# Attention 0: first scores and the spread of reciprocals on two row groups of TensorE, half of the normalisation on ScalarE and GpSimd, 24 transfers a step

## What is computed

```python
attn = jnp.einsum('bnchw,bncyx->bnhwyx', q, k) * (1.0 / np.sqrt(head_dim))
attn = jax.nn.softmax(attn, axis=-1)          # over x only: 32 keys of one row y
out = jnp.einsum('bnhwyx,bncyx->bnchw', attn, v).reshape(b, c, h, w)
out = jnp.einsum('oc,bchw->bohw', out_w, out) + out_b[None, :, None, None]
return out + input
```

## Time and profile before

| | |
|---|---|
| median of 3 runs | 3805.63 us (3801.79 to 3808.67) |
| profiled execution | 3806.82 us |
| its span (first to last instruction) | 3805.1 us |
| stage B in it | 106 to 958 us |
| PE busy over the span | 83% |
| DVE / ACT / POOL busy over the span | 50% / 74% / 8% |
| granted TensorE clock, mean | 0.956 of 2.4 GHz |

### The profile page before, as it was taken

One profiled execution on the slowest core, in us unless ns is written; L12 is line 12 of the kernel. 1 busy time (PEld: TensorE's weight loads), 2 busy tenths in 40 slices (PEclk: granted clock), 3 DMA queues, 4 the chain that ended last, 5 costly groups with the idle time before them and its releaser, 6 DMA issues.

```text
span 3805.1 us, 79261 instructions
## 1 busy us (share of the span) xinstructions
PE 3175.7 (83%) x27829; PEld 1180.1 (31%) x27829; DVE 1904.7 (50%) x2497; ACT 2817.5 (74%) x2759; POOL 300.4 (8%) x304
## 2 busy tenths in 40 slices
PE   5799999998773888888888888888888888779999
PEld 3344444444441222222222222222222222244443
DVE  3588878787575444444444444444444444452222
ACT  4444444444345999999999999999999999514555
POOL 5000000000354000000000000000000000001000
PEclk9899999999776999999999999999999999978999
DMA  5411111110143000000000000000000000200000
GB/s 186 115 40 47 48 44 47 48 32 10 38 144 124 17 16 17 17 17 17 17 17 17 17 16 16 16 17 17 17 17 17 17 17 16 72 17 6 11 14 14
DMA packets 118100, 134.09 MB, mean 35 GB/s; under 512 B 27246, under 2 KB 83660, under 8 KB 117964
## 3 DMA queue, kind: packets, MB, share of 16 engines
q1 hardware_dynamic: 117964, 132.29, 12.6%
HBM read 70.31 MB, written 55.57 MB: 33 GB/s over the span
## 4 chain that ended last, share of the span: by engine, by line
PE 57%; ACT 23%; issue 8%; DVE 5%; POOL 3%; SPq 1%; DMA 1%; ACTq 1%; DVEq 0%; POOLq 0%
ACT arena L878 22%; PE ps L1151 18%; PE ps L1128 10%; PE ps L989 3%; PE ps L1260 3%; PE ps L1267 3%; PE ps L1272 3%; PE ps L961 3%; PE ps L1007 2%; PE ps L1034 2%; PE ps L1009 2%; PE ps L1018 2%; DVE arena L1349 1%; POOL arena L698 1%; PE ps L1046 1%
## 5 line engine op out<-in xcount | busy, mean ns | idle before, releaser
L878 ACT ACTIVATE arena<-ps 128x1536 f32<-128x1536 f32 x1536 | 2063.8, 2095 | 11.0 <-PE ps L1128 11.0
L1151 PE MATMUL ps<-arena,Yall 128*32 128x512 f32 (+3 forms) x12288 | 1232.7, 496 | 10.8 <-POOL Yall L718 9.2
L1453 DVE TENSOR_TENSOR arena<-arena,causal 128x512 f32<-128x512 f32 x1024 | 674.3, 690 | 1043.4 <-ACT arena L878 1043.4
L1128 PE MATMUL ps<-Yall 15*128 15x512 bf16 (+3 forms) x6144 | 604.8, 330 | 396.7 <-ACT arena L878 373.8
L1128 PEld LDWEIGHTS ps<-Yall 15*128 15x128 bf16 x6144 | 163.2, 92 | 1277.3 <-ACT arena L878 1247.8
L803 ACT ACTIVATE arena<-ps 128x512 f32<-128x512 f32 x512 | 299.7, 595 | 293.3 <-PE ps L1009 283.8
L1151 PEld LDWEIGHTS ps<-arena,Yall 128*32 128x32 f32 x12288 | 284.1, 109 | 386.0 <-issue 360.4
L1349 DVE TENSOR_REDUCE arena<-ps 128x32 bf16<-128x1024 f32 x256 | 311.4, 1216 | 153.2 <-PE ps L989 153.2
L1356 DVE TENSOR_TENSOR arena<-arena,ps 128x512 f32<-128x512 f32 x512 | 329.2, 680 | 23.2 <-PE ps L1018 21.7
L1438 DVE COPY Yall<-ps 128x512 f32<-128x512 f32 x256 | 176.0, 688 | 198.3 <-PE ps L1151 198.3
L1009 PE MATMUL ps<-arena 128*128 128x256 bf16 x1024 | 257.5, 276 | 0.0
(11 more groups left out here) (172 smaller groups left out, 2083.8 us busy)
## 6 DMA issues: line engine op xcount, KB each, us to landing
Yall<-qstack SPq DMA_DIRECT2D x512, 30.0 KB
parts<-arena SPq DMA_DIRECT2D x8, 1536.0 KB, 5.9
arena<-parts SPq DMA_DIRECT2D x48, 256.0 KB, 5.4
arena<-parts SPq DMA_DIRECT2D x96, 128.0 KB, 2.8
Yall<-kstack SPq DMA_DIRECT2D x512, 24.0 KB
qstack<-arena SPq DMA_DIRECT2D x24, 384.0 KB, 3.2
attn<-Yall SPq DMA_DIRECT2D x512, 12.0 KB
arena<-arena SPq DMA_DIRECT2D x384, 16.0 KB, 1.8
```

The source lines that it names most:

```text
L878: act.activation(PR1[:, at:at + CW], bank(BPC * (kk % 2), BPC), ACT.Exp).then_inc(d_exp, 1)
L1128: mm = pe.matmul(bank(at + k)[:, s * P:(s + n) * P], Ks[par][HR * h:HR * h + QROWS, j * P:(j + 1) * P], Qs[par][HR * h:HR * h + QROWS, t * ...
L1151: mm = pe.matmul(o[HR * h:HR * (h + 1), :], Vg[par][:, j, 3 * h:3 * h + HR], pr[:, h * HALF + s * P:h * HALF + (s + n) * P], start=q < 2, ...
L1453: dve.tensor_tensor(v, v, m3, ALU.min).then_inc(d_mask, 1)
```

## The change

- First scores: two heads at once, one on array rows 0 to 31 (from `K1`), one on rows 32 to 63 (from `K2`), only the product of the high parts, half of the keys in each sub-step. Two matmuls of 512 columns as before, of 32 rows each.
- Spread: heads 0 and 1 on rows 0 to 47 into bank 4, heads 2 and 3 on rows 64 to 111 into bank 5; four matmuls of 48 rows and 256 columns in place of two of 96 rows and 512, all behind the first half of the scores. `RS` holds two half stacks, for the low and the high rows y.
- Normalisation: DVE multiplies heads 0 and 1 from bank 4. ACT copies bank 5 into one of two buffers in `sel`'s memory (`copy_spread`, between the two exponentials), and POOL multiplies heads 2 and 3 from there.
- Transfers: 24 of 16 partitions for each step, the 12 of the low rows y first, then the 12 of the high rows.
- ACT's exponentials stand ahead of the high and middle parts in sub-steps 3 and 4. POOL's low part stands in one list with its multiplications.
- POOL makes `sel` at the end of stage B, ahead of `V1`.

```diff
-        RS = [cut([NH0, QS], BF16) for _ in range(2)]
+        RS = [cut([2, 2, QS], BF16) for _ in range(2)]
...
+        spread_c = [flat_sel[:, k * HALF:(k + 1) * HALF] for k in range(2)]
+        spread = cut([SUB // 2, P], BF16)
...
@@ feed (SP)
-                    for r, part_made in enumerate((b_rhi, b_rmid, b_rlo)):
-
-                        sp.wait_ge(part_made, g + 1)
-                        for n in range(NH0):
-                            sp.dma_start(RS[st % 2][GK * r:GK * (r + 1), n, :], rec_parts[GK * n:GK * (n + 1), r, :])\
-                                .then_inc(rs_loaded[st % 2], INC)
+                    for y in range(2):
+                        for r, part_made in enumerate((b_rhi, b_rmid, b_rlo)):
+
+                            sp.wait_ge(part_made, g + 1)
+                            for n in range(NH0):
+                                to = P // 2 * (n // 2) + GH * r
+                                sp.dma_start(RS[st % 2][to:to + GH, y, n % 2, :],
+                                             rec_parts[GK * n + GH * y:GK * n + GH * (y + 1), r, :])\
+                                    .then_inc(rs_loaded[st % 2][y], INC)
@@ gpsimd
-            pool.memset(sel[0:NE, :, :], 0.0).then_inc(f_set, 1)
...
+            def pool_b(i, subs):
+                for k in subs:
+                    K = i * TURN + k
+                    if k % SUB == 4 and in_range(i, k, L_SUM + SUB + 2):
...
+                        pool.wait_ge(b_rmid, g + 1)
+                        wait_moved(pool, i, st - 1, 0)
+                        wait_moved(pool, i, st - 1, 1)
+                        pool.tensor_tensor(rec_parts[:, 2, :], rec_rest, rec_parts[:, 1, :],
+                                           ALU.subtract).then_inc(b_rlo, 1)
+                    if in_range(i, k, L_NORM):
+
+                        c = (k - L_NORM) % TURN
+                        e = E0[c // SUB % 2][:, c % SUB, 2:4, :].rearrange("p n q -> p (n q)")
+                        pool.wait_ge(b_copied, K + (1 - L_NORM))
+                        pool.tensor_tensor(e, e, spread_c[c % 2], ALU.mult).then_inc(b_norm_high, 1)
+            turns(pool, pool_b)
...
             pool.wait_ge(b_out, NSTEP)
+            pool.memset(sel[0:NE, :, :], 0.0).then_inc(f_set, 1)
...
             pool.memset(V1, 1.0).then_inc(ones_set, 1)
@@ scalar
+            def copy_spread(i, k, K):
+                if in_range(i, k, L_NORM):
+                    c = (k - L_NORM) % TURN
+                    act.wait_ge(b_spread_high, K + (1 - L_NORM))
+
+                    wait(act, b_norm_high, K + (-1 - L_NORM))
+                    act.activation(spread_c[c % 2], bank(5), ACT.Copy).then_inc(b_copied, 1)
@@ tensor
-                        for th in range(2):
-                            mm = pe.matmul(bank(th), Q1[q // 2][0:3 * D0, n, at:at + P],
-                                           half(K1[par][0:3 * D0, n, :], th), start=True, stop=True)
+                        for r, keys in enumerate((K1, K2)):
+                            mm = pe.matmul(bank(r), Q1[q // 2][D0 * r:D0 * (r + 1), n + r, at:at + P],
+                                           half(keys[par][D0 * r:D0 * (r + 1), n + r, :], th), start=True, stop=True)
...
-                        if in_range(i, k, L_NORM):
+                        if hp == 0 and in_range(i, k, L_NORM):
...
+                            for h in range(2):
+                                for G, made in enumerate((b_spread_low, b_spread_high)):
+                                    rows = slice(P // 2 * G, P // 2 * G + 3 * GH)
+                                    mm = pe.matmul(bank(4 + G)[:, h * QS:(h + 1) * QS], spread[rows, c % (SUB // 2), :],
+                                                   RS[c // SUB % 2][rows, c % SUB // (SUB // 2), h, :],
+                                                   start=True, stop=True)
...
-                        pe.wait_ge(b_norm, K * 2 + (2 - 2 * L_PV))
+                        pe.wait_ge(b_norm_low, K + (1 - L_PV))
+                        pe.wait_ge(b_norm_high, K + (1 - L_PV))
@@ vector
-                        for hp in range(2):
-                            e = E0[c // SUB % 2][:, c % SUB, 2 * hp:2 * hp + 2, :].rearrange("p n q -> p (n q)")
-                            dve.wait_ge(b_spread, K * 2 + (hp + 1 - 2 * L_NORM))
-                            dve.tensor_tensor(e, e, bank(4 + hp), ALU.mult).then_inc(b_norm, 1)
+                        e = E0[c // SUB % 2][:, c % SUB, 0:2, :].rearrange("p n q -> p (n q)")
+                        dve.wait_ge(b_spread_low, K + (1 - L_NORM))
+                        dve.tensor_tensor(e, e, bank(4), ALU.mult).then_inc(b_norm_low, 1)
```

More of the change, by code:

```diff
@@ L154, in hybrid_kernel @@
         sel = sb("sel", [P, NE, P])
+        flat_sel = sel[:, :, :].rearrange("p e c -> p (e c)")
         Yall = sb("Yall", [P, B, T])
@@ L203, in hybrid_kernel @@
         rec_parts = cut([3, QS], BF16)
-        maxima = cut([2 * NH0, GK], BF16)
-        spread = cut([NT, P], BF16)
+        maxima = cut([2, NH0, GK], BF16)
+        spread_c = [flat_sel[:, k * HALF:(k + 1) * HALF] for k in range(2)]
+        spread = cut([SUB // 2, P], BF16)
         window = cut([2 * GK - RB])
@@ L632, in _ @@
             constant(pool.tensor_copy(identb, ident[:, :]))
[L633 removed]
+            constant(pool.memset(spread, 0.0))
             constant(pool.memset(window, 0.0))
@@ L636, in _ @@
                 constant(pool.memset(K2[par][3 * GK:P], 0.0))
[L637 to L640, removed]
+            for r in (0, 1, 2, 4, 5, 6):
+                v = flat(spread).rearrange("p (y x) -> p y x", x=GK)
+                constant(pool.affine_select(out=v, in_=v, compare_op=ALU.not_equal, fill=1.0, base=-GH * r,
+                                            pattern=[[-1, GH], [0, GK]], channel_multiplier=1))
             for j in range(RB):
@@ L657, in _ @@
                                            ALU.subtract).then_inc(a_lo, 1)
[L660 to L670, removed]
-            pool.wait_ge(b_out, NSTEP)
+            def pool_b(i, subs):
+                for k in subs:
+                    K = i * TURN + k
+                    if k % SUB == 4 and in_range(i, k, L_SUM + SUB + 2):
+                        st = (k - L_SUM - SUB - 2) // SUB
+                        g = i * (2 * STEPS) + st
+                        pool.wait_ge(b_rmid, g + 1)
[9 more added lines that the diff above has]
+            turns(pool, pool_b)
+            pool.wait_ge(b_out, NSTEP)
+            pool.memset(sel[0:NE, :, :], 0.0).then_inc(f_set, 1)
+            pool.wait_ge(f_set, 1)
+            pool.affine_select(out=sel[0:NE, :, :], in_=sel[0:NE, :, :], compare_op=ALU.not_equal, fill=1.0,
+                               base=0, pattern=[[-1, NE], [0, P]], channel_multiplier=1).then_inc(f_set, 1)
+            pool.wait_ge(f_set, 2)
             pool.memset(V1, 1.0).then_inc(ones_set, 1)
@@ L804, in act_b @@
                                            bank(2 + hp), ACT.Exp, scale=SCALE0).then_inc(b_exp, 1)
+                            if hp == 0:
+                                copy_spread(i, k, K)
+                    else:
+                        copy_spread(i, k, K)
+                    if k % SUB == 3 and in_range(i, k, L_SUM + SUB + 1):
+                        st = (k - L_SUM - SUB - 1) // SUB
+                        act.wait_ge(b_rec, i * (2 * STEPS) + st + 1)
+                        wait_moved(act, i, st - 1, 0)
+                        wait_moved(act, i, st - 1, 1)
+                        act.activation(rec_parts[:, 0, :], rec, ACT.Copy).then_inc(b_rhi, 1)
+                    if k % SUB == 4 and in_range(i, k, L_SUM + SUB + 2):
+                        g = i * (2 * STEPS) + (k - L_SUM - SUB - 2) // SUB
+                        act.wait_ge(b_rrest, g + 1)
+                        act.activation(rec_parts[:, 1, :], rec_rest, ACT.Copy).then_inc(b_rmid, 1)
                     if k % SUB == L_OUT % SUB and in_range(i, k, L_OUT):
```

49 lines of the change are left out of this document (21 added, 28 removed).

## The result

| | before | after |
|---|---|---|
| median | 3807.15 us (4 runs, 3801.79 to 3809.89) | 3900.73 us (4 runs, 3895.92 to 3900.9) |
| ratio | | 1.0245, interval 1.0227 to 1.0262 |
| profiled execution / its span | 3806.82 / 3805.1 us | 3895.92 / 3894.2 us |
| eight sub-steps without a wait for queries | 24.9 to 25.0 us | 24.35 to 24.5 us in images 3, 5 and 7, 24.7 to 25.8 in 2, 4, 6 and 8 |

A forecast was written before the change was run, and what follows sets the result against it. PE bounds stage B, busy 96%. Steady part 3, queries 48.5 and 5.8, edges -3.8 and +3.2 sum to 56.7; 3806.8 + 56.7 - 1.2 gives 3862 us, range 3800 to 3915.

The forecast's parts named there:

- The queries: Image starts: query loads behind 24 transfers make PE wait 6.8 us; 48.5 us for five images, 5.8 for two.
- The 20 transfers: SP's queue behind ACT's middle part: 20 issues at 0.50 us each, done 10.0 us after sub-step 3 starts.
- rival (c): Stage B, dear on both: 0.14 us a change of tiling, 0.66 a transfer, wait 10.1; 3910 us, chance 0.11.
- The waits behind the loop's turns: Images 5 and 7: the loop's turn hides part of the query wait, leaving 2.9 us each, 5.8 in all.
- (a): Stage B: row-tiling changes nearly free, 0.03 us, and half-size transfers cost half; about 3785 us, chance 0.12.
- (b): SP's queue: only the transfers are cheap, 0.33 us; 3840 us, the forecast's lower side, within its chance of 0.67.
- (d): PE in stage B: row groups do not run together, so 3.52 us is not saved; 3964 us, chance 0.04.
- The steady groups: Eight sub-steps of stage B: -3.52 streaming, +2.20 tiling changes, +0.55 and +0.88 waits, sum +0.1; +3 us over 29 groups.
- The wait for the product's copy: PE at k = 0 modulo 8 waits for ACT's copy: from 0.81 to 1.36 us, +0.55.
- The wait for POOL: PE in sub-step 5 wants POOL's product at 5.37 us, sees it at 6.25: new wait of 0.88.
- The edges: Stage B's ends: first nine sub-steps -3.8 us; `sel` ahead of stage C and POOL's last product +3.2.
- Rival (e): Image starts: queries come in time, 20 issues in under 3.2 us; 3808 us, no change, chance 0.06.

The follow-up runs named there:

- kernel 1: The changed kernel with the six loads of the next image's low-half queries issued ahead of the step's 24 transfers: 3811.74 us, 1.001 of before.
- kernel 11: kernel 1 with the high and middle parts made ahead of ACT's exponentials and the spread directly behind the first scores: 3781.25 us, 0.9932 of before.
- kernel 6: kernel 1 with the spread moved directly behind the first scores, one change of tiling less in each sub-step: 3850.72 us, 1.0113 of before.
- kernel 2: The kernel before plus 12 unused 16-partition transfers of a constant in each step, ahead of the query loads: 3876.36 us, 1.0184 of before.
- kernels 5, 10 and 12: kernel 1 with both products on DVE: 3810.23 us; also parts ahead of exponentials, `sel` at the start: 3784.72; that plus spread behind first scores: 3787.28.

## Why the prediction was right in kind and short in size

**The queries: right mechanism, mis-sized.** They were to cost 54.3 us (48.5 and 5.8) over a kernel that already waits 4.5 for them, so 58.8 against a kernel that doesn't wait at all; that one is kernel 1, and against it they cost 89. The terms, at the third image, counted from the start of sub-step 3 (280.23 us):

- The middle part was ready at 6.4 us (286.19 + 0.43, said 6.75), the loads took 5.46 from issue to use (said 5.4), PE wanted them at 15.2 (said 15.3). All good.
- *The 20 transfers took 13.1 us (to 299.73), not 10.0.* That is the term that was mis-sized: I took 0.50 us for a transfer of 16 partitions, from the slope of 5 ns a partition between the issues of rows 9. They start 0.63 us apart. The issues of rows 9 are of another kind, so their slope said nothing of these. The line of the transfers has the same median after as before, 589 and 590 ns:

```profile
L486 SPq DMA_DIRECT2D arena<-arena x768: 507/589/1949, 146.4 to 1030.8; - x192
```
```profile
L478 SPq DMA_DIRECT2D arena<-arena x384: 507/590/1810, 153.0 to 943.3; - x192
```

  So the wait was 9.8 us instead of 6.8. The upper end (0.66, wait 10.1) was nearly the true one, and I had it as half of rival (c). That rival's 3910 lies nearer to the result than my 3862, but by luck: its other half, 0.14 for a change of tiling, was wrong and put 25 us in the place of what it lacked.
- *The waits behind the loop's turns.* I gave them 2.9 us each, and they are 8.37 and 8.07. The same mis-sized term makes 3.1 of the difference. The rest is that the series of transfers itself is longer there:

```profile
506.23 19.02 SPq L486 DMA_DIRECT2D arena<-arena  x24
525.52 2.80 SPq L472 DMA_DIRECT2D arena<-parts  x6
```

  19.02 us for 24 instead of 16.58. Single issues are longer: those at 510.32, 518.60 and 522.31 us take 1.27, 1.77 and 1.68 us, where one in the series of the third image took 1.12 and the others 0.6 or less. The one at 518.60 falls into PE's turn and the one at 522.31 stands right behind it; the seventh image has the same pattern. SP's own turn is not among them: it comes two steps later, between 591 and 599 us. What lengthens the issues is not shown. PE is back from its turn at 521.87 and waits until 530.62. The turn hides what I said it would, 3.9 us: 2.9 + 3.1 + 2.4 is the 8.4 measured.
- The clock behind the wait: 16.32 us from the first scores at 305.19 to those of the fourth sub-step after, where 12.49 are usual (358.07 to 370.56). That is 3.8 us, as predicted. The prediction took it from the one stretch behind the loop's turn.

Five waits of 9.8 with 3.8 of clock are 68, the two turns 16.4: some 84.5 of the measured 89. About 4 us stay unexplained.

**PE's own work: right.** Plain sub-step 2.75 (said 2.73), first scores 0.32, spreads 0.32, a change of tiling 0.10, also for the 48-row pairs for which no row of before stood. The Trainium skill, "TensorEngine Tiling (Array Packing)", Key Properties, says that a change of the tiling mode drains the engine. The trace agrees: 0.10 us is lost at each change, for row tiles as for column tiles. Rivals (a), (b) and (d) are out: the changes cost 0.10, the transfers 0.63, and the pairs do run together, four matmuls of 256 columns in 0.22 and the change.

**The steady groups: near in sum, by errors that cancel.** Said +0.1 for eight sub-steps, measured -0.6 in the fast groups. The wait for the product's copy became 1.14, not 1.36: on ACT the copy starts 336.70 - 335.25 = 1.45 us after the first exponential, where I had 1.08 + 0.54 = 1.62, since three large ones in a row follow each other closer than the end of the last suggested. The wait for POOL became 0.47, not 0.88: PE wanted the product at 5.39 us (said 5.37), and it was there at 5.86 (said 6.25), since the middle and low parts were ready 0.2 to 0.3 earlier and POOL's two products take 2.51 in a row.

```profile
335.25 0.60 ACT L816 ACTIVATE arena<-ps 128x512 f32<-128x512 f32 x1 [0.85 <-PE ps L1037]
335.75 0.59 ACT L790 ACTIVATE sel<-ps 128x512 f32<-128x512 f32 x1
336.23 0.60 ACT L816 ACTIVATE arena<-ps 128x512 f32<-128x512 f32 x1
336.70 0.40 ACT L835 ACTIVATE Yall<-ps 128x256 f32 x1
```
```profile
286.69 0.67 POOL L671 TENSOR_TENSOR arena<-arena 128x256 bf16<-128x256 f32 x1 [3.06 <-ACT arena L831]
287.32 2.51 POOL L678 TENSOR_TENSOR arena<-arena,sel 128x512 f32<-128x512 f32 x2
```

The first fence is ACT with the product's copy, the second POOL in sub-step 4.

By that, stage B should have gained 29 x 0.6 = 18 us. It did not, and *here a step was missing*: I called the 12 transfers of the high rows hidden and never asked when the 12 of the low rows land, which PE uses first. In two of three steps they land after sub-step 7 wants them, mostly by 0.3 to 0.7 us, at most 3.1:

```profile
293.31 0.39 PE L1050 MATMUL ps<-arena 48*128 48x256 bf16 x4 [0.31 <-DMA arena<-arena]
```

Those waits are 22.1 us, 5.4 before: 16.7 of the 18. Kernel 7 shows their cause: it makes the two parts ahead of the exponentials, changes nothing else against kernel 1, and they fall from 19.7 to 6.4. So it is the late parts and not the number of transfers, which is 24 in both. For everything but the queries, steady part and edges, +2.4 was said; the chain above has -32 + 7 + 34 = +9. That the sum came so near is luck: a gain of 18 us that I did not see stood against a wait that I did not see either.

**The edges: right.** From the first to the tenth first scores of stage B 18.72 us pass (104.44 to 123.16), 22.24 before: -3.5 (said -3.8). `sel` cost a wait of 2.82 at the start of stage C, which with POOL's last product was to be 3.2.

**Rival (e)**, the queries in time, was given 3808 us; kernel 1 makes that case and runs in 3811.7. As an account of the changed kernel it fell, as its condition said.

## What to carry to other kernels

Cutting each of these transfers into halves doubled the time of the queue that issues them, 7.9 to 16.6 us. Count what stands behind it in that queue, up to the next load that an engine needs, and put that load first: here six loads moved by 24 places were worth 89 us of 3900. A diff with five parts has five prices: the one good part (32 us) and the one that nobody would list as a part at all (two small ACT instructions moved behind two large ones, 34 us) were found only by taking them one at a time. And where PE is the pace and a helper's chain ends a wait, taking work off PE ahead of that wait returned nothing (kernel 11), and in kernel 6 it came with longer waits elsewhere, a lower clock and 39 us more.

## What the runs showed of the hardware

- A transfer inside SBUF costs SP 0.59 us busy and 0.63 us from one to the next, 0.66 to 0.69 on average over a step's series with its waits for the parts, for 32 partitions and for 16 alike, whether from the reciprocals or from a constant (kernel 2). Other transfers, of 15 and 3 partitions, take 328 and 267 ns; which property makes them half as dear is not shown.
- DVE's subtraction of two SBUF tiles (128x256, the rest of the reciprocals) takes 418 ns in the kernel before and much longer where POOL multiplies the spread reciprocals: median 810 in the changed kernel, 1470 in kernel 7. In kernels 5, 10 and 12, which leave POOL's product out, it is back at 416 to 418. First the changed kernel, then kernel 7, then before (ns min/median/max):

```profile
L1401 DVE TENSOR_TENSOR arena<-arena x32: 410/810/1287, 146.4 to 1016.3; 128x256 f32<-128x256 f32 x32
```
```profile
L1404 DVE TENSOR_TENSOR arena<-arena x32: 409/1470/1473, 146.7 to 896.3; 128x256 f32<-128x256 f32 x32
```
```profile
L1366 DVE TENSOR_TENSOR arena<-arena x32: 408/418/420, 153.5 to 937.0; 128x256 f32<-128x256 f32 x32
```

  DVE's products that read PSUM are not touched: 680 ns before, 681 after.
- A wait of 1.49 us for the product's copy in each step came with a clock of 0.95 in kernel 6 (240 to 340 us), where each step also held a wait for POOL of 0.81 or more and one for transfers of 0.65 to 1.69. In kernel 11 it stood in the same place with a wait for transfers of 0.20 to 0.56 beside it and none for POOL, and the clock was 1.00. From what sum or spacing of waits on the clock falls can't be said from these runs.
